# Two copies moved ahead in ScalarE's queue, and a tap subtraction cut to a 29 by 29 region

## What is computed

```python
x = x + spectral_conv(_ln_c(x), L0_conv_kernel_base)      # FFT, 32 x 32 modes mixed over channels, inverse FFT
t = _to_tokens(x)                                          # 32768 tokens of 64 channels
t = t + moe(_ln_t(t), L0_ffn_router_w, ..., L0_ffn_expert_b)
x = _from_tokens(t, x)
x = x + depthwise_conv(_ln_c(x), L1_conv_kernels)          # 29 x 29 taps per channel, 'SAME'
t = _to_tokens(x)
t = t + moe(_ln_t(t), L1_ffn_router_w, ..., L1_ffn_expert_b)

def moe(x, router_w, router_b, expert_w, expert_b):        # 8 experts, the best 2
    router_probs = softmax(x @ router_w + router_b)
    top_p, top_i = top_k(router_probs, 2)
    top_p = top_p / sum(top_p)
    expert_out = einsum("bnd,edc->bnec", x, expert_w) + expert_b
    return sum over the two of top_p * gathered expert_out
```

## Time and profile before

| | us |
|---|---|
| median of 3 runs | 964.58 |
| lowest and highest of them | 963.37, 965.38 |
| the profiled execution's own time | 966.94 |
| the span of its trace | 965.1 |

### The profile page before, as it was taken

The page is one execution under the profiler, slowest core; times in us unless marked ns, Lnnn a source line. Parts: engine busy times, 40 slices in busy tenths (PEclk is TensorE's granted clock), DMA queues, the critical chain, the costliest instruction groups (busy, mean ns, idle before and its releaser), DMA issues.

```text
span 965.1 us, 24392 instructions
## 1 busy us (share of the span) xinstructions
PE 854.9 (89%) x9482; PEld 701.7 (73%) x9482; DVE 774.8 (80%) x1421; ACT 506.2 (52%) x1051; POOL 568.8 (59%) x504
## 2 busy tenths in 40 slices
PE   6996788677999999996899999999568999999998
PEld 6986777645676666654899999999536666667665
DVE  5767698878899999999787677765788899997884
ACT  2477385786666666311344444343278566676411
POOL 3770203157788887796654334420226788888888
PEclk9996577878999999999899999999859999999999
DMA  9988100103677777673787877787000010101101
GB/s 378 346 286 260 49 1 2 40 14 155 271 304 288 293 291 294 275 314 126 263 281 258 283 269 254 259 282 261 1 1 23 23 45 23 44 27 41 45 35 53
DMA packets 48291, 163.09 MB, mean 169 GB/s; under 512 B 9424, under 2 KB 9936, under 8 KB 46032
## 3 DMA queue, kind: packets, MB, share of 16 engines
q1 hardware_dynamic: 48208, 161.96, 46.3%
HBM read 93.46 MB, written 68.49 MB: 168 GB/s over the span
## 4 chain that ended last, share of the span: by engine, by line
PE 55%; DVE 24%; POOL 6%; issue 6%; ACT 5%; DMA 3%; SPq 1%; POOLq 0%; DVEq 0%; ACTq 0%
PE pair L1692 24%; DVE R L904 7%; PE pair L1619 7%; PE pair L1605 5%; PE pair L1606 5%; PE pair L1616 4%; DMA X<-x_rows 3%; PE pair L1492 3%; POOL R L571 3%; ACT pair L1249 2%; DVE R L660 2%; DVE R L833 2%; DVE R L844 2%; PE pair L1583 2%; DVE work L660 2%
## 5 line engine op out<-in xcount | busy, mean ns | idle before, releaser
L904 DVE TENSOR_TENSOR R<-pair,R 128x896 f32<-128x896 f32 x256 | 275.3, 1083 | 50.8 <-PE pair L1606 50.0
L571 POOL TENSOR_TENSOR R<-R 128x768 f32<-128x768 f32 x128 | 231.9, 1811 | 94.4 <-DVE R L904 78.4
L1692 PE MATMUL pair<-R 128*128 (+4 forms) x2880 | 227.6, 243 | 9.2 <-DVE R L982 9.2
L1692 PEld LDWEIGHTS pair<-R 128*128 128x128 f16 x2880 | 224.9, 98 | 12.1 <-issue 9.5
L1249 ACT ACTIVATE pair<-X,work 128x64 f32<-128x64 f32 x480 | 166.6, 394 | 124.1 <-DVE R L844 121.6
L1605 PE MATMUL pair<-work,R 128*128 128x448 f16 x512 | 185.8, 363 | 24.7 <-DVE R L904 24.5
L1606 PE MATMUL pair<-work,R 128*128 128x448 f16 x512 | 184.9, 361 | 0.0
L581 POOL TENSOR_TENSOR R<-R 128x512 f32<-128x512 f32 x128 | 164.7, 1286 | 10.0
L997 DVE COPY R<-R 128x1152 f32<-128x1152 f32 x64 | 92.7, 1449 | 65.3 <-PE pair L1692 64.6
L1367 ACT COPY R<-R 128x1152 f32<-128x1152 f32 x64 | 82.0, 1282 | 117.3 <-PE pair L1692 117.3
L1619 PE MATMUL pair<-R,ident_sb 128*128 128x256 f32 x496 | 130.3, 386 | 0.0
(11 more groups left out here) (137 smaller groups left out, 1292.8 us busy)
## 6 DMA issues: line engine op xcount, KB each, us to landing
taps_halves<-R SPq DMA_DIRECT2D x128, 458.5 KB, 3.3
R<-taps_halves SPq DMA_DIRECT2D x64, 917.0 KB, 4.7
X<-x_tok SPq DMA_DIRECT2D x4, 2048.0 KB, 18.1
out<-X SPq DMA_DIRECT2D x15, 512.0 KB, 2.6
R<-spec_pairs SPq DMA_DIRECT2D x16, 272.0 KB, 5.3
X<-x_rows SPq DMA_DIRECT2D x4, 1024.0 KB, 11.0
R<-x_chan SPq DMA_DIRECT2D x4, 1024.0 KB, 14.0
X<-x_rows SPq DMA_DIRECT2D x2, 2048.0 KB, 27.2
```

The lines of the kernel that those rows point to most:

```text
L571: pool.tensor_tensor(pr[:, :, 192:384], pr[:, :, 0:192], pr[:, :, 192:384], ALU.add).then_inc(half_ready, 1)
L904: dve.tensor_tensor(pr.rearrange("p t (e c) -> p t e c", c=C), pair[p % 2][:, :].rearrange("p (t e c) -> p t e c", t=2, c=C)[:, :, 0:NE - ...
L1692: mm = pe.matmul(acc[:, y0:y1, x0:x1, :], blocks[i % 2][:, ks, 2 - y, 1 - x, :], src[:, y0 + y:y1 + y, x0 + x:x1 + x, :], start=(ks == 0 a ...
```

## The change

There are two parts.

1. In ACT's `start_chunk`, `copy_parts` now stands ahead of the first half of a `normalise` of the same p, and behind the second half of the one begun at p - 1. START_NORMS and START_TURNS share p = 3 and p = 5, so two copies move, of parts (1, 1) and (1, 2), in each layer. At all other p the order stays.
2. `taps_low` works on the 29 by 29 region alone, 841 columns in place of 2412. The columns around it are zero in the high halves, so they were and stay zero in the low ones.

```diff
@@ -947,7 +947,10 @@
                 dve.wait_ge(taps_step, 1)
                 r = BLOCKS[1]
-                dve.scalar_tensor_tensor(out=taps_16[r], in0=taps_f32[r], scalar=TAP_SCALE, in1=taps_16[r],
+                first = CENTRE - KS // 2 * (PITCH + 1)
+                f32, f16_ = (m[r, first:first + KS * PITCH].rearrange("p (x y) -> p x y", y=PITCH)[:, :, 0:KS]
+                             for m in (taps_f32, taps_16))
+                dve.scalar_tensor_tensor(out=f16_, in0=f32, scalar=TAP_SCALE, in1=f16_,
                                          op0=ALU.mult, op1=ALU.subtract).then_inc(taps_step, 1)
@@ -1319,15 +1322,15 @@
                 for p in range(NPAIR):
                     if p % 4 == COPY_AT and p >= 4 * SUM_LAG:
                         copy_sum(layer, 0, p // 4 - SUM_LAG)
-                    if p in START_NORMS:
-                        k, j = START_NORMS[p]
-                        normalise(layer, k, k % 2, j, range(0, 4))
                     if p - 1 in START_NORMS:
                         k, j = START_NORMS[p - 1]
                         normalise(layer, k, k % 2, j, range(4, 8))
                     if p in START_TURNS:
                         k, j = START_TURNS[p]
                         copy_parts(layer, k, k % 2, j)
+                    if p in START_NORMS:
+                        k, j = START_NORMS[p]
+                        normalise(layer, k, k % 2, j, range(0, 4))
```

## The result

| | before | changed |
|---|---|---|
| median, us | 965.47 | 959.81 |
| lowest to highest of 15 runs each, us | 962.95 to 968.11 | 957.80 to 962.86 |
| the profiled execution's own time, us | 966.94 | 957.80 |
| its span, us | 965.1 | 956.0 |

The ratio of the times is 0.9943, with a 95% interval of 0.9932 to 0.9954. The change saves 5.66 us where 5.4 was forecast. The changed kernel's profiled execution is the fastest of its 15.

The account below looks back on a forecast made before the run. PE, then DVE at the gates, was taken to bound the layers' opening chunks. 1.34 + 0.5 + 1.65 + 0.6 + 1.34 = 5.4 us takes the median from 964.58 to 959.2 us, range 956.4 to 962.3.

Parts of the forecast that it names:

- The taps: Layer 0, chunk 0: tap subtraction falls from 3.58 to 1.93 us, 0.91 of it waiting for POOL; saves 1.65 us.
- The rival of dear rows: Tap subtraction: 29 strided rows cost as much as L950 did, so the taps give nothing; 961.9 us, chance 0.04.
- The copy at p = 3: Chunk 0, each layer: earlier copy of part (1, 1) moves the next turn and PE's queue forward; saves 1.34 us per layer.
- The copy at p = 5: Chunk 0: copy of part (1, 2) comes 2.2 us earlier, but beside other work; worth nothing unless PE gets faster.
- The clock in that stretch: PE behind the turn of part (1, 2): shorter idle keeps its clock up; 0.5 us in layer 0, 0 in layer 1.
- the walk: DVE's queue followed with its own durations if PE's clock holds: p = 10 starts about 216.9, 2.5 us earlier than 219.38.
- The clock behind the gates: Layer 0, after the last gate: shorter taps starve PE less, so its clock recovers; 0.6 us of 0 to 1.17.
- that rival: PE's clock stays up at all three places, both layers' openings and behind the taps; 956.0 us at best, chance 0.16.
- the slower case: Later, steady chunks: shifted gaps make PE's clock fall where it held; six falls give 967.3 us, chance 0.04.
- moved slow stretch: Chunk 0: PE's clock falls earlier too, costing up to 0.8 us more per layer; 961.9 us, chance 0.12.
- PE's idle time before the turn of part (1, 2): Sign, chunk 0: from the last product of p = 5 to this turn about 1.3 us in layer 0, before 2.70.
- DVE's wait before p = 6: Sign, chunk 0 of layer 0: DVE's idle time is near 0.6 us instead of 1.91; the same in layer 1.

Follow-up runs that it names:

- e4: Changed kernel with the tap subtraction one pair later, at p = 14 instead of 13; median 958.40 us, ratio 0.9944 to the kernel before.
- e8: Changed kernel with the first copy of the sums at p = 8 and the tap subtraction at p = 14; median 957.42 us, ratio 0.9928.
- e7: Changed kernel with the tap subtraction on 1102 adjoining columns instead of 841 in 29 pieces; single run 960.04 us.
- e5: Changed kernel with only the copy at p = 3 moved ahead, the one at p = 5 as before; ratio 0.9989 to the kernel before.
- e10: The kernel before, unchanged, run once more for a second trace; 965.64 us.
- e2: Kernel before with both copies moved ahead but the tap subtraction still on 2412 columns; median 960.70 us, ratio 0.9968.
- e3: Changed kernel with ACT's first copy of the sums at p = 8 instead of 9; median 957.48 us, ratio 0.9948 to the kernel before.
- e11: The changed kernel, unchanged, run once more for a second trace; 957.25 us.
- e6: Changed kernel with only the copy at p = 5 moved ahead, the one at p = 3 as before; ratio 0.9983 to the kernel before.
- e12: Kernel of e8 with PE's route one pair later in chunk 1 of each layer alone; 953.33 us, ratio 0.9883 to the kernel before.
- e9: Kernel of e8 with PE's first three route parts one pair later in every chunk but the first; median 957.16 us, ratio 0.9921.

## Why the prediction was right, and where it was not

**The time.** 959.2 was forecast, 959.81 measured, a saving of 5.66 us where 5.4 was said. The places named were the ones at work, but within the order's part the terms were assigned wrongly and made up for each other, so part of the nearness is luck. The two traced executions save 7.7 us in these places, not 5.4, and no trace of a median execution exists to settle the difference.

**The taps, a saving right to 0.01 us.** L953 took 1.95 us (forecast 1.93), 13 to 14 fell by 1.64 (forecast 1.65), and L581 beside it took 1.94 (forecast 2.0). Both inner parts are shown: the wait by e4 and e8 (1.11 and 1.03 us without it), the price of a column by e7. The rival of dear rows falls.

**The copy at p = 3, 1.34 us in each layer: a wrong step.** The turn did move, but e5 shows that this copy alone leaves PE waiting at the next turn instead.

**The copy at p = 5, "worth nothing": wrong.** The prediction reasoned at PE's pace of before, where the turn of part (1, 3) came after the copy in either kernel. But the edit at p = 3 changes that pace. In e5 the same turn comes 7.29 us after p = 4 (211.11 - 203.82), in the changed kernel 5.04 (207.84 - 202.80): 2.25 us hang on the second copy once the first is early. The sentence that it "matters if PE gets faster" was there, and its price was not put into the sum. The pair was worth 1.61 and 1.44 us in the traces, 3.05 together, against 1.34 + 0.5 + 1.34 = 3.18; against e10 it was worth 3.8.

**The clock in that stretch, 0.5 of up to 1.15 us.** The clock did stay up in both layers of the two traces: 208 to 210 is at 1.00, though layer 1's gap before the turn is still 1.81 us. The forecast for layer 1, that a gap of 2 us would keep it down, was wrong for these, though the clock did fall there in e2, e4 and e7. Nor could the full 1.15 us come: the walk let p = 10 start at 216.9 against 219.38, 2.5 us gained, because it left out PE's sum, which waits for ACT's copy of the sums (L1294). That wait holds 4 to 10 at 13.68 us, a gain of 1.61. e3 removes it and gets 12.72, 2.57 us less than before (2.11 less than e10): the walk's 2.5 was about right for a kernel without that wait.

**The clock behind the gates, 0.6 us in layer 0 and nothing in layer 1: mis-sized.** The first pair of traces has 1.33 and 1.66, the second (e10 and e11) 0.22 and 2.87. The medians allow less: of 5.66 us, 4.69 are in the other terms of the first pair (1.61 + 1.44 + 1.64), which leaves 1.0. The term of the taps in layer 0 is near 0.6 only with the new order: 6.92 us in e2, with long taps, against 6.18 in the changed kernel. In layer 1 it is the order alone that brings the gain. I found 4.68 or 4.69 in the changed kernel, e2, e4, e7 and e11, 5.89 to 6.26 in e3, e5, e6 and e8, and 6.33 to 7.56 with the order of before. So the value goes with the kernel more than with the execution. What decides between these values the traces don't show. e12 shows the way out: with the route out of the wait the step is 3.19, in both layers and both kernels that have it (e9, e12).

**The rivals.** In both traced executions the clock stayed up behind the turn in both layers and behind the gates of layer 1, and in part in the fourth place, and these executions lie at 957.25 and 957.80, toward that rival's 956.0; the median stays at the forecast. No steady chunk changed its step, so the slower case has nothing for it. No moved slow stretch is seen in the changed kernel. It is in e5, though: in layer 0 it costs more than the edit gives.

**The signs that were named.** PE's idle time before the turn of part (1, 2) is 0.86 us ("about 1.3" was said). Counted from p = 4 the turn starts at 0.78 us (203.58 - 202.80) where 0.91 was expected (205.00 - 204.09), so its place held and the idle time was sized too long. In layer 1 the idle time is 1.81 us where 2.01 was said. DVE's wait before p = 6 is zero instead of 0.6, since PE's clock stayed up behind the turn. 0 to 2 in layer 0, with L904 of p = 0 at 231.01 right behind the last gate, is 6.18 where 6.2 to 7.4 was said.

## What to carry to other kernels

When one engine is freed at one place, walk its queue on at the new pace to the next thing that it waits for, over every queue that feeds it (here the second copy and the copy of the sums): two edits may be worth nothing apart and 3 us together. The same holds for e8: behind the wait that was removed stood another copy of the sums. When the wait of the critical engine is for a result whose consumer has slack, put work that needs nothing in front of it, and only in the pass that has the wait: in all passes the same move gave most of its gain back, 0.3 to 0.4 us each time. Where TensorE's clock sets a step, one trace of it is a sample: take the size from medians, and look for an edit that keeps TensorE busy through the wait.

## What the runs showed of the hardware that I had not expected

- By itself, how long PE had idled did not decide whether its clock fell. In layer 1 of the changed kernel a gap of 1.81 us at the turn left it at full speed, and so did 1.79 us in e6 (layer 0). In layer 1 of e4, with the same order on ACT, 1.54 us at the same turn was followed by a mean of 0.65. Behind the gates of layer 1 the gap is 2.20 or 2.21 us in both kernels, and the clock after it 0.73 before and 1.00 in the changed kernel (744.70 to 749.30, above). The turn and the window behind it, in the changed kernel and then in e4:

```profile
719.29 0.61 PE L1586 MATMUL pair<-ident_sb,R 128*128 128x128 f16 x8 [1.81 <-ACT R L1282]
...
719.30:723.00 3.70, 3.70 (x45) 2.89 (x46) 2.58 (x7) 3.61 (x11) 3.31 (x8) 1.00 0.00 0
...
719.20 0.61 PE L1586 MATMUL pair<-ident_sb,R 128*128 128x128 f16 x8 [1.54 <-ACT R L1282]
...
719.20:722.90 3.70, 3.70 (x37) 2.98 (x38) 2.59 (x7) 3.61 (x11) 3.31 (x8) 0.65 0.00 0
```

- The time of an execution goes with this clock. Over the 15 runs of the changed kernel the time falls as the mean granted clock rises, with a correlation of -0.84: 957.80 us at 0.937, 962.86 at 0.930. For the kernel before it is -0.82 and -0.69 over two sets of 23 runs. That shows that they go together, not in which stretch the time is lost.
- A short POOL instruction waits as long as DVE's has left to run: L548, 0.25 us of work, took 1.04 us in e4 while L953 ran, and L552 took 1.06 in e8.
- A region of 29 rows of 29 columns, 38 apart, costs DVE what its 841 columns cost, 1.03 us where L571 is not in its way (e8).
